# The expert stage of an attention and mixture-of-experts kernel: its convolution-kernel chunks in nine steps instead of eight, the exponential a step later, expert numbers read ahead

## The chip, the core and the metric

The kernel runs on one core of a Trainium2 chip. A core has five engines with a queue of instructions each: TensorE (PE in the profile; PEld is its weight load), VectorE (DVE), ScalarE (ACT), GpSimd (POOL) and SyncE (SP, which here only issues DMAs). They wait for one another by semaphores. The metric is the time of one execution in microseconds on the device; less is better.

## The reference, cut to what matters

Two layers, each a cross attention and a mixture of experts, on x of shape (2, 1024, 256). The stage that the change touches holds the experts of layer 0 (1) and, in the same loop, the convolution kernel K of the state-space part of layer 1 (2), which depends on parameters alone.

```python
# (1) two of eight experts for each of 2048 tokens
topk_val, topk_idx = jax.lax.top_k(gate_scores, TOP_K)
...
for e in range(E):
    h = jnp.einsum('btd,hd->bth', x, W1[e]) + b1[e]
    a, b = jnp.split(h, 2, axis=-1)
    g = a * jax.nn.sigmoid(b)
    eo = jnp.einsum('bth,dh->btd', g, Wo) + bo
    out = out + eo * comb[..., e:e + 1]
# (2) 256 channels, 64 states, 1024 positions
dtA = dt[:, None] * A
dC = C * (jnp.exp(dtA) - 1.0) / A
powers = jnp.exp(dtA[:, :, None] * jnp.arange(L))
K = 2.0 * jnp.einsum('dn,dnl->dl', dC, powers).real
```

## The kernel before

The program is written out engine by engine; the order in each queue is the order of the code, and nothing is scheduled.

**Expert steps.** The 4096 token-expert pairs are sorted by expert and padded to ST = 39 tiles of 128 rows. Each engine runs a loop over `st`, in which step u = st handles tile u:

- GpSimd gathers the rows of tile st from scr_z in device memory by an indirect DMA (line 1554; two buffers, so it waits until TensorE has turned tile st - 2). Then it scatters the gated rows of tile u = st - 4 to scr_g (line 1563), for which it waits for VectorE's product of that tile. At each even st from 4 to 34 it also multiplies and adds a bias to one tile of X (lines 1574 and 1576, the bias pair). At st = 27 it clears VW (a memset).
- TensorE reads the expert number of the tile from teI into a register (`value_load`, line 737), waits for ScalarE's copy of the turned rows and, two steps back, for VectorE's product (g_ready), runs six matmuls into two banks, and then turns (transposes) the gathered tile u + 2 (line 727), for which the gather must have landed.
- ScalarE takes the sigmoid of one bank (line 1261) and copies the turned tile u + 2 (line 1097).
- VectorE multiplies the other bank by it (line 2061), the gating product. It writes one of two buffers, so it also waits until the scatter of tile u - 2 has landed.

**Convolution kernel.** Between these steps K is built in KCH = 4 chunks. With `c, part = (st - KOFF) // KPARTS, (st - KOFF) % KPARTS` each engine does some part of chunk c in step st; before, KOFF = 2 and KPARTS = 8. Before the first chunk VectorE computes coefficients in three blocks (`more_coefficients`). In each chunk:

- parts 0 and 1: VectorE computes two arrays of angles (turns, four operations each). ScalarE takes two sines of each array in parts 1 and 2 (lines 1275 and 1276);
- GpSimd's part 5 writes the arguments of the exponentials, two products (line 1584). GpSimd's st runs some three steps ahead of the others, since it gathers ahead. It waits until the small products of the chunk before are done;
- part 3: ScalarE takes the two exponentials (line 1281);
- parts 4 to 7: VectorE multiplies sines, exponentials and coefficients, ten products, the last at line 2101;
- parts 0 and 1 of the next chunk: TensorE runs the small products, 128 matmuls with tiles of 64 by 32 in each of two halves, behind the expert step and its turn. ScalarE copies each half to KT in that step; the second half needs the first copied, since they use one bank.

Sigmoid, sine and exponential have different tables in ScalarE: each change between them is a load (ACT_TABLE_LOAD at the line of the function that follows). Chunk 0's small products stand at st = 10, 11, those of chunk 3 at st = 34, 35.

**Behind the loop.** SyncE waits for all eight halves to be copied and writes KT to scr_k (line 436), then waits for the last scatter and loads the gated rows from scr_g, four MB-sized pairs (line 311); VectorE sums each tile's two rows, TensorE turns and projects them. TensorE in the meantime computes the film products, which also wait until the eight halves are copied.

Of the kernel before, what the change touches and what calls it, by code (L numbers as in the profile page):

```python
# [29 lines left out]
NE, HID0 = 8, 512  # L30
# [10 lines left out]
FLOOR = -0.5 + 1.0 / 512  # L41
KCH, KPARTS = 4, 8
KOFF = 2
KW = 32
# [41 lines left out]
def build(nc, d, out, last="F"):  # L86
    ctx = ExitStack()
    with ctx:
# [394 lines left out]
        def _(pe):  # L483
# [206 lines left out]
            if "B" in stages:  # L690
# [41 lines left out]
                turn_x(1)  # L732
                pe.wait_ge(s["te_ready"], 1)
                for st in range(max(ST, KOFF + KCH * KPARTS + 2)):
                    if st < ST:
                        u = st
                        e = pe.value_load(teI[0:1, u:u + 1], min_val=0, max_val=NE - 1)
                        pe.wait_ge(s["xTg_sb"], u + 1)
                        if u >= 2:
                            pe.wait_ge(s["g_ready"], u - 1)  # L740
                        for half in range(2):
                            cols = slice(half * HID0, (half + 1) * HID0)
                            o = bank(2 * (u % 2) + half)

                            mm(o, picked[:, u:u + 1].broadcast_to([BROWS, P]), b1r[:, cols], True, False)
                            for k in range(KD):
                                ins = mm(o, xTg[:, u % 2, k, :],
                                         w1all[:, k, bass.ds(e, 1), cols].rearrange("p o n -> p (o n)"), False, k == KD - 1)
                        ins.then_inc(s["h_ps"], 1)
                        if u + 2 < ST:  # L750
                            turn_x(u + 2)
# [341 lines left out]
        def _(a):  # L1093
# [129 lines left out]
            if "B" in stages:  # L1223
# [31 lines left out]
                for st in range(max(ST, KOFF + KCH * KPARTS + 2)):  # L1255
# [15 lines left out]
                    if 0 <= c < KCH and part in (1, 2):  # L1271
# [5 lines left out]
                            .then_inc(s["k_sin"], 1)  # L1277
                    if 0 <= c < KCH and part == 3:
                        a.wait_ge(s["kv_arg"], 2 * c + 2)
                        for mag in (Pr, Qr):  # L1280
                            a.activation(mag, mag, ACT.Exp).then_inc(s["mag_ready"], 1)
# [185 lines left out]
        def _(p):  # L1467
# [72 lines left out]
            if "B" in stages:  # L1540
# [9 lines left out]
                for st in range(ST + SCAT):  # L1550
# [26 lines left out]
                    c, part = (st - KOFF) // KPARTS, (st - KOFF) % KPARTS  # L1577
                    if 0 <= c < KCH and part == 5:

# [139 lines left out]
        def _(v):  # L1719
# [128 lines left out]
            if "B" in stages:  # L1848
# [206 lines left out]
                for st in range(max(ST, KOFF + KCH * KPARTS)):  # L2055
# [17 lines left out]
                    if c >= KCH:  # L2073
                        continue
                    if st in (1, 4, 5):
                        more_coefficients((1, 4, 5).index(st))
                    if c < 0:
                        continue
                    if part < 2:
                        ang = tk[2 * part]  # L2080
                        tts(quads(ang), chan(TURN, c), ramps[:, part, :].unsqueeze(1).unsqueeze(1).broadcast_to([P, 2, 16, R]), ALU.mult)
                        turns4(ang, tk[2 * part + 1]).then_inc(s["k_trig"], 1)
                    elif part == 4:
                        v.wait_ge(s["k_sin"], 2 * c + 2)
# [4 lines left out]
                        tts(flat(Pr), flat(Pr), tk[1], ALU.mult)  # L2089
                    elif part == 5:  # L2090
                        tt(quads(tk[0]), quads(flat(Pi)), chan(17, c), ALU.mult)
                        tt(quads(tk[1]), quads(flat(Pr)), chan(17, c), ALU.mult)
                        v.tensor_tensor(flat(Qr), flat(Qr), tk[3], ALU.mult).then_inc(s["k_used"], 1)
                        own.settle()
                    elif part == 6:
                        tt(quads(flat(Pr)), quads(flat(Pr)), chan(16, c), ALU.mult)
                        tt(quads(flat(Pi)), quads(flat(Pi)), chan(16, c), ALU.mult)
                        own.settle()
                    elif part == 7:
                        tts(flat(Pr), flat(Pr), tk[0], ALU.subtract)  # L2100
                        v.tensor_tensor(flat(Pi), flat(Pi), tk[1], ALU.add).then_inc(s["k_used"], 1)
# [548 lines left out]
```

## Time and profile before

| | us |
|---|---|
| median of 3 runs (765.82 to 771.96) | 769.88 |
| the profiled execution | 768.24 |
| its span from first to last instruction | 766.4 |
| busy: TensorE / VectorE / GpSimd / ScalarE | 662.7 / 542.7 / 381.5 / 313.4 |
| the expert loop, from the first expert matmul to the last | 175.8 to 375.4 |

The profile gives for each instruction its start in us from the start of the span, its length, the line of the code, what it writes and reads, and for the time in which its engine stood idle before it the instruction that ended the wait. "issue" is a wait for nothing that the profile shows. A timeline merges repeats (x128).

### The profile page before, as it was taken

How to read it: one execution, taken by the hardware profiler on the slowest of the kernel's cores; microseconds unless marked ns; L12 is line 12 of the kernel's file. 1: busy time of each engine (PE TensorE's matmuls, PEld its weight loads, DVE VectorE, ACT ScalarE, POOL GpSimd, SP SyncE). 2: the span in 40 equal slices, each digit the busy share in tenths (PEclk: the TensorE clock that was granted, in tenths of full speed). 3: DMA queues.
4: the chain of work that ended last, by engine and by line, in shares of the span. 5: the costliest groups of instructions: out<-in, count | busy, mean ns of one | idle time of the engine just before them, and what ended most of it. 6: DMA issues, size and time to landing. Idle time of an engine off the chain costs nothing.

```text
span 766.4 us, 10944 instructions
## 1 busy us (share of the span) xinstructions
PE 662.7 (86%) x3432; PEld 375.1 (49%) x3432; DVE 542.7 (71%) x1678; ACT 313.4 (41%) x690; POOL 381.5 (50%) x463
## 2 busy tenths in 40 slices
PE   5779998728999999999988779978997999899993
PEld 3434545614445354545467534434543654657672
DVE  5878885393994765744468899999975994745472
ACT  2645764302827465462122467777113220031411
POOL 3777775024988787874213457887300210212130
PEclk9979998657999999999999989999799999999997
DMA  7950001012122212212496000110100000000011
GB/s 216 335 195 18 28 1 56 28 55 69 62 83 84 82 65 83 85 63 88 133 378 254 2 0 2 62 50 0 56 0 0 2 0 1 0 0 1 1 55 56
DMA packets 32958, 52.67 MB, mean 69 GB/s; under 512 B 8712, under 2 KB 21451, under 8 KB 32645
## 3 DMA queue, kind: packets, MB, share of 16 engines
q1 hardware_dynamic: 27620, 36.36, 14.2%
q0 software_dynamic: 4992, 15.34, 5.8%
q8 instruction: 29, 0.48, 0.3%
q10 hardware_dynamic: 288, 0.26, 0.1%
q14 instruction: 29, 0.23, 0.1%
HBM read 36.48 MB, written 15.47 MB: 68 GB/s over the span
## 4 chain that ended last, share of the span: by engine, by line
PE 48%; DVE 29%; ACT 8%; POOL 6%; issue 5%; DMA 3%; SPq 1%; DVEq 0%; POOLq 0%; ACTq 0%
PE ps L485 43%; DVE arena L2236 6%; DVE arena L2226 4%; DVE arena L1723 4%; DVE kp L1723 2%; POOL arena L1528 2%; ACT L1261 2%; PE ps L544 1%; DVE arena L2061 1%; ACT arena L1097 1%; DMA arena<-scr_g 1%; DVE arena L345 1%; PE ps L797 1%; ACT L1275 1%; DVE arena L1998 1%
## 5 line engine op out<-in xcount | busy, mean ns | idle before, releaser
L485 PE MATMUL ps<-arena 64*32 64x32 f32 (+10 forms) x2346 | 478.0, 391 | 19.2 <-DVE arena L1998 8.7
L485 PEld LDWEIGHTS ps<-arena 64*32 64x32 f32 (+7 forms) x2346 | 227.0, 151 | 201.4 <-issue 159.4
L1097 ACT ACTIVATE arena<-ps 128x512 f32<-128x512 f32 (+4 forms) x253 | 121.1, 494 | 239.0 <-PE ps L485 116.0
L340 POOL TENSOR_SCALAR rstd<-mv 128x1 f32<-128x1 f32 (+2 forms) x33 | 13.1, 397 | 218.5 <-DVE mv L334 164.6
L2061 DVE TENSOR_TENSOR arena<-ps,arena 128x512 f32<-128x512 f32 x39 | 26.9, 689 | 76.9 <-ACT arena L1261 75.1
L1563 POOL DMA_INDIRECT scr_g<-arena,destU x39 | 49.5, 1269 | 37.4 <-DVE arena L2061 28.2
L1554 POOL DMA_INDIRECT arena<-scr_z,idsU x39 | 49.1, 1259 | 22.7 <-PE ps L727 10.8
L1261 ACT ACTIVATE arena<-ps 128x512 f32<-128x512 f32 x39 | 23.3, 598 | 85.6 <-PE ps L485 85.4
L2236 DVE MATCH_REPLACE8 arena<-arena 128x77 f32<-128x77 f32 x256 | 53.9, 219 | 0.0
L1417 ACT ACTIVATE arena<-ps,b1p 128x512 f32<-128x512 f32 x32 | 22.0, 687 | 74.3 <-PE ps L485 74.3
L2226 DVE MAX8 arena<-arena 128x8 f32<-128x77 f32 x256 | 41.5, 222 | 1.1 <-ACT arena L1307 1.1
L1723 DVE TENSOR_TENSOR arena<-arena 128x1024 f32<-128x1024 f32 (+8 forms) x44 | 40.2, 913 | 0.9
L1723 DVE TENSOR_TENSOR arena<-arena,kp 128x1024 f32<-128x1024 f32 (+1 forms) x36 | 39.4, 1113 | 0.6
L1528 POOL TENSOR_TENSOR arena<-arena 128x616 f32<-128x616 f32 x32 | 38.9, 1218 | 0.0
L485 PE MATMUL ps<-b1r,picked 73*128 73x512 bf16 x78 | 30.4, 389 | 9.1 <-DVE arena L2061 4.7
L544 PE MATMUL ps<-ident,arena 128*128 128x128 f32 (+1 forms) x160 | 25.7, 294 | 12.1 <-POOL arena L1528 8.0
L1820 DVE TENSOR_REDUCE arena<-ps 128x8 f32<-128x616 f32 x32 | 25.2, 787 | 11.9 <-PE ps L485 11.5
L485 PE MATMUL ps<-wof,arena 128*128 128x256 f32 x128 | 30.8, 386 | 0.0
L342 POOL TENSOR_TENSOR rstd<-rstd,neghalf 128x1 f32<-128x1 f32 (+2 forms) x33 | 29.2, 886 | 2.8
L544 PEld LDWEIGHTS ps<-ident,arena 128*128 128x128 f32 (+1 forms) x160 | 17.4, 144 | 25.9 <-POOL arena L1528 13.0
L1188 ACT ACTIVATE arena<-arena 128x616 f32<-128x616 f32 x32 | 22.9, 715 | 11.9 <-DVE arena L1824 11.9
L345 DVE TENSOR_SCALAR arena<-X,mv,rstd 128x256 f32<-128x256 f32 x48 | 19.3, 454 | 11.2 <-POOL rstd L342 11.2
(223 smaller groups left out, 995.1 us busy)
## 6 DMA issues: line engine op xcount, KB each, us to landing
arena<-in_w1t SPq DMA_DIRECT2D x8, 1024.0 KB, 13.8
arena<-scr_g SPq DMA_DIRECT2D x8, 1024.0 KB, 8.1
scr_z<-arena SPq DMA_DIRECT2D x4, 512.0 KB, 2.9
arena<-in_c_dftf SPq DMA_DIRECT2D x1, 2048.0 KB, 16.0
arena<-in_L_xattn_W SPq DMA_DIRECT2D x2, 1024.0 KB, 6.3
out<-X SPq DMA_DIRECT2D x14, 128.0 KB, 1.8
X<-in_x SPq DMA_DIRECT2D x2, 512.0 KB, 4.8
X<-in_x SPq DMA_DIRECT2D x1, 1024.0 KB, 7.6
```

Source lines behind the costliest of these rows:

```text
L342: p.tensor_tensor(rstd[:, at:at + n], rstd[:, at:at + n], neghalf[:, 0:n], ALU.pow).then_inc(s[signal], 1)
L485: return pe.matmul(o, l, r, start=first, stop=final)
L544: ins = pe.transpose(o, Pb[:, u % PBUF, c * P:c * P + m], ident[:])
L1097: return a.activation(o, i, ACT.Copy)
L1261: a.activation(sig[:, u % 2, :], bank(2 * (u % 2) + 1), ACT.Sigmoid).then_inc(s["sig_ready"], 1)
L1528: p.tensor_tensor(pv, pv, smA[:, u % PBUF, :].unsqueeze(2).broadcast_to([P, HG, S2]), ALU.mult)\
L1554: p.indirect_dma_start(xg[:, st % 2, :], None, scr_z, bass.IndirectOffsetOnAxis(ap=idsU[:, st:st + 1], axis=0))\
L1563: p.indirect_dma_start(scr_g, bass.IndirectOffsetOnAxis(ap=destU[:, u:u + 1], axis=0), gt[:, u % 2, :], None).then_inc(s[f"gs{u % 2}"], 16)
L1723: own.done(v.tensor_tensor(o, x, y, op))
L2061: v.tensor_tensor(gt[:, u % 2, :], bank(2 * (u % 2)), sig[:, u % 2, :], ALU.mult).then_inc(s["g_ready"], 1)
L2226: own.done(v.max(top[:, par, h, 8 * r:8 * r + 8], hv(cur)[:, h, :]))
L2236: ins = v.match_replace(hv(Rr)[:, h, :], top[:, par, h, 8 * r:8 * r + 8], hv(cur)[:, h, :], TAKEN)
```

## The change

Three edits to the loop, and the coefficients' places go with them.

1. KPARTS goes from 8 to 9 and KOFF from 2 to 1. Chunk c begins at st = 1 + 9c instead of 2 + 8c. The small products of chunks 0 to 3 follow their step at st = 10, 19, 28, 37 (first halves) and 11, 20, 29, 38; before, 10, 18, 26, 34 and 11, 19, 27, 35. The coefficients move from st = 1, 4, 5 to 0, 3, 4.
2. The exponentials move from part 3 to part 4, GpSimd's arguments from part 5 to 6, VectorE's products from parts 4 to 7 to parts 5 to 8. The sines stay in parts 1 and 2.
3. TensorE reads the next step's expert number behind its own expert matmuls, in front of the turn and the small products.

```diff
-KCH, KPARTS = 4, 8
-KOFF = 2
+KCH, KPARTS = 4, 9
+KOFF = 1
...
+                def expert_of(u):
+                    return pe.value_load(teI[0:1, u:u + 1], min_val=0, max_val=NE - 1)
+
+                following = expert_of(0)
                 for st in range(max(ST, KOFF + KCH * KPARTS + 2)):
                     if st < ST:
                         u = st
-                        e = pe.value_load(teI[0:1, u:u + 1], min_val=0, max_val=NE - 1)
+                        e = following
...
                         ins.then_inc(s["h_ps"], 1)
+                        if u + 1 < ST:
+                            following = expert_of(u + 1)
                         if u + 2 < ST:
                             turn_x(u + 2)
...
-                    if 0 <= c < KCH and part == 3:
+                    if 0 <= c < KCH and part == 4:
                         a.wait_ge(s["kv_arg"], 2 * c + 2)
...
-                    if 0 <= c < KCH and part == 5:
+                    if 0 <= c < KCH and part == 6:
 
                         p.wait_ge(s["kp_par"], 1)
...
-                    if st in (1, 4, 5):
-                        more_coefficients((1, 4, 5).index(st))
+                    if st in (0, 3, 4):
+                        more_coefficients((0, 3, 4).index(st))
...
-                    elif part == 4:
+                    elif part == 5:
                         v.wait_ge(s["k_sin"], 2 * c + 2)
...
-                    elif part == 5:
+                    elif part == 6:
...
-                    elif part == 6:
+                    elif part == 7:
...
-                    elif part == 7:
+                    elif part == 8:
```

GpSimd's queue at the arguments of chunk 1, before, from the gather at st = 15 on (arena<-scr_z is a gather, scr_g<-arena a scatter; the line numbers are those of the kernel before):

```order
L1554 DMA arena<-scr_z,idsU 128x256
L1563 DMA scr_g<-arena,destU 9088x512
L1584 TENSOR_TENSOR arena<-kp,ramps 128x1024 x2
L1554 DMA arena<-scr_z,idsU 128x256
L1563 DMA scr_g<-arena,destU 9088x512
L1574 TENSOR_SCALAR arena<-rows,cw 128x256
L1576 TENSOR_TENSOR X<-X,arena 128x256
L1554 DMA arena<-scr_z,idsU 128x256
```

The same stretch after the change, whose line numbers are 7 or more higher:

```order
L1561 DMA arena<-scr_z,idsU 128x256
L1570 DMA scr_g<-arena,destU 9088x512
L1561 DMA arena<-scr_z,idsU 128x256
L1570 DMA scr_g<-arena,destU 9088x512
L1581 TENSOR_SCALAR arena<-rows,cw 128x256
L1583 TENSOR_TENSOR X<-X,arena 128x256
L1591 TENSOR_TENSOR arena<-kp,ramps 128x1024 x2
L1561 DMA arena<-scr_z,idsU 128x256
```

The two products of the arguments moved behind one more gather and scatter and behind a bias pair. In chunk 0 they stay where they are, at st = 7.

ScalarE's queue in chunk 1, before, from the copy of a turned tile (128x256) in part 2 on, between the two sine pairs:

```order
L1097 ACTIVATE arena<-ps 128x256
L1275 ACT_TABLE_LOAD
L1275 ACTIVATE arena<-arena 128x1024
L1276 ACTIVATE arena<-arena,halfpi 128x1024
L1261 ACT_TABLE_LOAD
L1261 ACTIVATE arena<-ps 128x512
L1097 ACTIVATE arena<-ps 128x256
L1281 ACT_TABLE_LOAD
L1281 ACTIVATE arena<-arena 128x1024 x2
L1261 ACT_TABLE_LOAD
L1261 ACTIVATE arena<-ps 128x512
L1097 ACTIVATE arena<-ps 128x256
```

After the change:

```order
L1104 ACTIVATE arena<-ps 128x256
L1282 ACT_TABLE_LOAD
L1282 ACTIVATE arena<-arena 128x1024
L1283 ACTIVATE arena<-arena,halfpi 128x1024
L1268 ACT_TABLE_LOAD
L1268 ACTIVATE arena<-ps 128x512
L1104 ACTIVATE arena<-ps 128x256
L1268 ACTIVATE arena<-ps 128x512
L1104 ACTIVATE arena<-ps 128x256
L1288 ACT_TABLE_LOAD
L1288 ACTIVATE arena<-arena 128x1024 x2
L1268 ACT_TABLE_LOAD
```

The exponentials (the line with x2) stand behind one more sigmoid and copy; the loads in front of the two sine pairs have not moved against the sigmoids there.

TensorE's queue at step 10 and the first small products, before, from the step's last matmul on (32x32 x64 is how the small products stand here):

```order
L485 MATMUL ps<-arena 128x512
L727 MATMUL ps<-ident,arena 128x128 x2
L485 MATMUL ps<-arena 32x32 x64
L737 TENSOR_LOAD teI
L737 ISA x2
L485 MATMUL ps<-b1r,picked 128x512
```

After the change:

```order
L485 MATMUL ps<-arena 128x512
L736 TENSOR_LOAD teI
L736 ISA x2
L727 MATMUL ps<-ident,arena 128x128 x2
L485 MATMUL ps<-arena 32x32 x64
L485 MATMUL ps<-b1r,picked 128x512
```

The read of the expert number (TENSOR_LOAD) moved from behind the small products to in front of the turn.

## Rows read from the trace of the kernel before

**Rows 1.** Busy us (count) of PE, PEld, DVE, ACT, POOL in two stretches.

```profile
237.00:255.30 18.30, 16.73 (x48) 7.75 (x48) 5.79 (x8) 18.12 (x21) 13.57 (x12) 1.00 0.21 73
255.30:269.30 14.00, 12.82 (x37) 5.70 (x37) 13.86 (x14) 2.84 (x7) 12.50 (x9) 1.00 0.21 75
```

**Rows 2.** Timeline, PE: start us, length us, instruction, idle before and its releaser.

```profile
228.02 2.23 PE L485 MATMUL ps<-arena 64*32 64x32 f32 x128 [0.77 <-DVE arena L2101]
230.53 0.38 PE L485 MATMUL ps<-b1r,picked 73*128 73x512 bf16 x1 [0.27 <-issue]
...
237.24 0.38 PE L485 MATMUL ps<-b1r,picked 73*128 73x512 bf16 x1 [0.28 <-issue]
...
241.35 0.38 PE L485 MATMUL ps<-b1r,picked 73*128 73x512 bf16 x1
...
255.35 0.38 PE L485 MATMUL ps<-b1r,picked 73*128 73x512 bf16 x1 [1.23 <-DVE arena L2061]
...
269.30 2.23 PE L485 MATMUL ps<-arena 64*32 64x32 f32 x128 [0.72 <-DVE arena L2101]
...
355.13 3.20 PE L485 MATMUL ps<-arena 128*128 x4 [0.60 <-issue]
...
373.49 1.88 PE L485 MATMUL ps<-arena 128*128 x4
```

**Rows 3.** Timeline, ACT, of the same chunk.

```profile
237.01 1.07 ACT L1097 ACTIVATE arena<-ps 64x512 f32<-64x512 f32 x1 [1.52 <-PE ps L485]
238.09 1.28 ACT L1275 ACT_TABLE_LOAD   x1
...
241.50 1.28 ACT L1261 ACT_TABLE_LOAD   x1
...
249.27 1.28 ACT L1281 ACT_TABLE_LOAD   x1
...
252.59 1.28 ACT L1261 ACT_TABLE_LOAD   x1
```

**Rows 4.** Timeline, DVE, of the same chunk.

```profile
254.51 0.69 DVE L2061 TENSOR_TENSOR arena<-ps,arena 128x512 f32<-128x512 f32 x1 [4.81 <-ACT arena L1261]
...
267.86 1.38 DVE L2101 TENSOR_TENSOR arena<-arena 128x1024 f32<-128x1024 f32 x1
```

**Rows 5.** Timeline, POOL, of the same chunk.

```profile
240.44 3.92 POOL L1584 TENSOR_TENSOR arena<-kp,ramps 128x1024 f32<-128x1024 f32 x2
...
245.83 0.99 POOL L1563 DMA_INDIRECT scr_g<-arena,destU  x1 [0.31 <-issue]
246.86 0.95 POOL L1574 TENSOR_SCALAR arena<-rows,cw 128x256 f32<-128x256 f32 x1
...
248.77 1.03 POOL L1554 DMA_INDIRECT arena<-scr_z,idsU  x1 [0.15 <-issue]
...
255.48 1.72 POOL L1563 DMA_INDIRECT scr_g<-arena,destU  x1 [3.08 <-DVE arena L2061]
...
266.94 1.68 POOL L1574 TENSOR_SCALAR arena<-rows,cw 128x256 f32<-128x256 f32 x1
...
269.99 1.90 POOL L1554 DMA_INDIRECT arena<-scr_z,idsU  x1 [0.16 <-issue]
```

**Rows 6.** DMA issues of the page: KB each, median us from issue to landing.

```profile
scr_k<-arena SPq DMA_DIRECT2D x4, 256.0 KB, 5.0
...
arena<-scr_z,idsU POOLq DMA_INDIRECT x39, 3.2
```

**Rows 7.** Busy us by stretch as in rows 1, then PEclk, DMA share, GB/s.

```profile
356.00:357.00 1.00, 1.00 (x2) 0.34 (x1) 0.00 (x0) 0.00 (x0) 0.00 (x0) 0.50 0.34 135
```

**Rows 8.** Timeline, SPq (SyncE's queue of DMA issues) and DVE, end of the experts.

```profile
364.21 4.50 SPq L436 DMA_DIRECT2D scr_k<-arena  x4
379.89 17.48 SPq L311 DMA_DIRECT2D arena<-scr_g  x8
...
388.30 0.49 DVE L1726 TENSOR_SCALAR arena<-arena,cw 128x512 f32<-128x512 f32 x1 [2.65 <-DMA arena<-scr_g]
```

## The prediction

> **What bounds it now.** I first read the busy shares of the expert stage in stretches [rows 1], cut at the three places where the limiting engine changes. One chunk of the convolution kernel lasts from one first half of its small products to the next, 228.02 to 269.30 [rows 2]: 41.28 us for eight expert steps, and three such periods stand in the stage. From 237 to 255.3 ScalarE is busy 18.12 of 18.30 us; from 255.3 to 269.3 VectorE 13.86 of 14.00 and GpSimd 12.50. TensorE is nearly full everywhere, but a step costs it only 4.11 us with its turn (237.24 to 241.35) and a half of the small products 2.23 [rows 2]. Below, C is the start of a first half, and steps are counted from the expert step in front of it, step 0: in the chunk shown step 0 is st = 10 of the code, step 4 is st = 14. What is called a loop index is st itself.
>
> ScalarE [rows 3] copies the second half out (237.01, 1.07), does the first sine pair with its table load (238.09 to 241.50: 3.41), a sigmoid with load and copy, the second pair and another sigmoid (241.50 to 249.27: 7.77, so 2.18 for each sigmoid), the exponentials with their load (249.27 to 252.59: 3.32), and one more load of 1.28, so that the sigmoid of step 4 starts at 253.9, C+25.9. VectorE's gating product of that step starts at 254.51 [rows 4], and TensorE's step 6 waits 1.23 for it [rows 2]. VectorE then works without a pause up to the end of its last product, 254.51 to 267.86+1.38: 14.7 us, and the next small products start right behind it. So each chunk pays a ScalarE queue and a VectorE queue one behind the other. GpSimd waits once, 3.08 us at its scatter of step 4 [rows 5].
>
> **What changes, in numbers.** Removed: nothing; the counts of matmuls, table loads, products and DMAs stay. All is in the order.
>
> *First chunk.* The coefficients and the turns start a step earlier. GpSimd's argument keeps its place, loop index 7, in chunk 0, so the gathers stay where they are. TensorE waited 0.77 for VectorE in front of the first half at 228.02 [rows 2]; the coefficients no longer stand in front of the products that end there, so this goes, and so does one issue gap like the 0.27 in front of 230.53. I take -1 us; bounds 0 (the wait becomes one for a gather) and -2 (twice that, if VectorE's earlier steps had pushed others).
>
> *Steady chunk without GpSimd.* The expert number is read behind the step's matmuls, under cover of the array's work, so the 0.27 in front of 230.53 [rows 2] goes; the second half ends at C+2.23+4.2+2.23 = C+8.7. If it were exposed somewhere else, it would cost the same 0.27 a step, 10 us over 39 steps at worst; I see no such place, since the array has several matmuls queued there. ScalarE: copy 1.07, sines 3.41, load 1.28, so the sigmoid of step 2 starts at C+14.5 and its product is ready at C+15.9. After a second pair the sigmoid of step 3 starts at C+20.1, and step 5 still waits about 0.5. Now no exponential stands in front of step 4's sigmoid: it starts at C+21 instead of C+25.9. The exponentials run C+22 to C+25.3, step 5's sigmoid at C+26.6. Its product and the 14.7 us behind it end at C+41.9. TensorE alone needs C+8.7 and eight steps of 4.11, C+41.6, with the wait C+42.1. So nine steps would take 42.2, against 46.4 for nine at the old pace.
>
> *GpSimd in that chunk.* This is what I expect to take part of it back. Its arguments (240.44, 3.92) now stand at loop index 16: no longer behind the scatter of step 1 but behind the scatter of step 2 and a bias pair. That scatter needs the product that the sines delay, C+15.9; it starts at C+16.1. From there GpSimd has no pause: scatter and bias pair 2.94 (245.83 to 248.77), arguments 3.95, a gather (1.03), a scatter (0.99) and a gather with 0.3 in front of each DMA, 3.9 in all, and the scatter of step 4 starts at C+26.9, hardly before the old C+27.46. In the old trace it was 14.5 us from that scatter to the start of the gather of index 21 (255.48 to 269.99), which took 1.90 [rows 5]; all of a gather lands 3.2 us after issue by the median [rows 6], and I put 3.7 here, since this one is 0.9 longer than the short 1.03. So it lands at C+45.1, and the turn of step 9, after which the small products now come, ends at C+45.5. Before, that gather was needed a step after the products. The arguments themselves are ready at C+23, just in time for the exponentials, which need them at C+23.3. The first period is thus 45.5, not 42.2. The second has one bias pair less there but VW's memset: 45. In the third the bias pairs run out at loop index 34, and 42.2 stands.
>
> The price of a GpSimd instruction is the open one: the bias multiply took 0.95 at 246.86, while VectorE was idle, and 1.68 at 266.94, while it ran products of two tensors [rows 5]. [...] By the short prices the stretch of 14.5 shrinks to 3 scatters and 2 gathers at 1.3 and 2 pairs at 1.9, 10.3 us, the gather lands by C+41 and GpSimd doesn't bind: 42.2. By the long ones (1.9 for each of the DMAs, 3.05 for a pair as from 266.94 to 269.99) it is 17, and a period is 48. I take the measured 14.5, since the same VectorE products lie beside it again.
>
> *End of the stage.* The last first half stands in step 37 instead of 34, so from C only 2.23 and 4.0 are left to the end of step 38: 6.2. Old: 228.02 to 373.49+1.88 = 375.4, 147.4 us. New: 45.5+45+42.2+6.2 = 138.9. Of the 8.5, some 2 are a spell at half clock in the old trace, which I don't repeat: four matmuls took 3.20 at 355.13, against 1.88 at 373.49, with 0.50 granted [rows 2, 7], so 1.3 more in that half of a step, and I count 2 for the step with its gaps.
>
> *Tail.* The kernel's write-out to scr_k is issued when the last half is copied. It took SyncE 4.50 us at 364.21, under cover of the last steps [rows 8]. Now that half follows step 38: ready 2.25 (products) + 1.1 (copy) after the step's end, issued until 7.9 after it. Behind it on SyncE stands the load of the gated rows, which before was issued 4.5 after the end (379.89). So it is at least 3.4 late. The rows of scr_k, 256 KB in 5.0 by the median [rows 6], still run into that load; both bounds: 3.4 (no collision) and 7.3 (the load moves nothing until the last of the four writes has landed, 5.0 behind an issue at 6.8). I take 4.5, nearer the lower end, since only the last write overlaps. The Trainium skill (DMA: Bandwidth & Descriptors, Specifications) wants pieces of 512 B for full rate, and these are 256 B; scr_k's 5.0 for 256 KB agrees. At the rate of the gated load there would be no collision, and the sum 1 us lower. VectorE's first sum (388.30, behind 2.65 us of waiting for that load) moves with it, so all of it is on the path. The film products on TensorE move too, by 2.7, and have cover: they ended well before 388.
>
> **Sum.** -1 - 8.5 + 4.5 = -5.0 on the profiled execution's 768.24: 763.2. The median of the three runs, 769.88, stands 1.6 above it; with that, 764.9. I say 765.0.
>
> **Rivals.**
> *GpSimd does not bind* (chance 0.25). For it: GpSimd still waits 3.08 in each chunk now [rows 5]. Against: 12.50 of 14.00 busy in the VectorE stretch. Periods of 42.2: another 6.1 off, 758.8 on the median's scale.
> *Slower: TensorE loses its clock in the new waits* (0.09). Place: the turn in front of the small products, where it waits about 3 us for the gather in two chunks. In the old trace the granted clock was at 0.50 (1.2 of 2.4 GHz) in the stretch at 356, after a step broken by gaps behind small products [rows 2, 7]. One such fall cost about 2 us there. Three of them eat the 5.0, and with them ScalarE's queue starts later too; six make it over 1% slower. Against: the waits of 1.23 within steps did not lower it.
> *It does not do what it says* (0.08): the sines, which stay back to back, hold the period, the exponential only moves ScalarE's load from one step to the next, and TensorE's saving is returned by the tail: 768 to 771.
>
> **Chances.** The forecast has 0.58, within 762 to 769. A measurement of this kernel can tell about 1%, 7.7 us. Faster by more, below 762.2: nearly all of the first rival and a little of the forecast's edge, 0.27. Slower, above 777.6: half of the second rival, 0.05. The rest, 0.68, is within 1%. Range 757 to 772: from the first rival with the short tail to long GpSimd prices in both chunks (+5) and a tail of 6.5 to 7.3.
>
> **What would show it.** Right: three periods between first halves, of about 45.5, 45 and 42; ScalarE's sigmoid of the fourth step some 5 us earlier after C; TensorE's longest idle times in front of the turn before a first half, released by the gather; GpSimd's arguments right behind a scatter and bias pair that waited for VectorE; no issue gap behind small products; SyncE's gated load 8 us behind the last expert step. Wrong: periods of 42 (GpSimd was mispriced); idle TensorE released by VectorE's last product (ScalarE and VectorE still bind); granted clock of 0.50 inside the stage; the first sum no later after the last step than now, 13 us.

## The result, and the profile after the change

| us | before | after | predicted |
|---|---|---|---|
| median of 4 runs beside each other | 769.20 (765.82 to 771.96) | 778.33 (775.82 to 781.59) | 765.0 (757 to 772) |
| the profiled execution, its span | 768.24, 766.4 | 779.91, 778.1 | 763.2 |
| first small products of chunk 0 | 228.02 | 227.30 | 227.0 |
| the three periods from there | 41.28, 41.06, 41.13 | 47.70, 48.31, 44.13 | 45.5, 45, 42.2 |
| last first half to the end of the last gating product | other order | 10.74 | 7.56 |
| from there to the first sum | 11.57 | 17.66 | 16.1 |
| the first sum | 388.30 | 395.84 | 383.3 |

The ratio is 1.011, with a 95% interval of 1.007 to 1.015: slower, and outside my range. The last column is worked out from the prediction's terms: 6.2 plus the 1.36 by which the last product ended behind TensorE before (376.04 + 0.69 against 373.49 + 1.88), 11.57 plus 4.5, and 388.30 less 5.0. The miss at the first sum is 12.5 us: 0.3 in the start, 7.4 in the periods, 3.2 in the last steps, 1.6 in the tail.

Timeline of PE after the change (columns as in [rows 2]):

```profile
205.73 0.38 PE L485 MATMUL ps<-b1r,picked 73*128 73x512 bf16 x1 [3.10 <-DVE arena L2068]
...
227.30 2.24 PE L485 MATMUL ps<-arena 64*32 64x32 f32 x128
...
248.79 0.38 PE L485 MATMUL ps<-b1r,picked 73*128 73x512 bf16 x1 [0.51 <-DVE arena L2068]
...
274.63 0.44 PE L727 MATMUL ps<-ident,arena 128*128 128x128 f32 x2 [3.17 <-DMA arena<-scr_z,idsU]
275.00 2.77 PE L485 MATMUL ps<-arena 64*32 64x32 f32 x124
...
279.11 3.62 PE L485 MATMUL ps<-arena 128*128 x4
...
285.06 2.23 PE L485 MATMUL ps<-arena 64*32 64x32 f32 x128
...
318.60 0.44 PE L727 MATMUL ps<-ident,arena 128*128 128x128 f32 x2 [2.08 <-DMA arena<-scr_z,idsU]
...
367.44 3.00 PE L485 MATMUL ps<-arena 64*32 64x32 f32 x128 [1.93 <-DVE arena L2108]
370.37 0.61 PE L485 MATMUL ps<-b1r,picked 73*128 73x512 bf16 x1
370.77 3.62 PE L485 MATMUL ps<-arena 128*128 x4
```

The first period ends with a turn, at 274.63, that waits 3.17 for the gather, as I had said; but the four matmuls at 279.11 behind it then take 3.62 instead of 1.88. The third ends with a first half, at 367.44, that waits 1.93 for VectorE's last product (L2108), and the same follows. The busy time by stretch (columns as in [rows 1], then PEclk, DMA share, GB/s) shows why:

```profile
255.30:275.00 19.70, 14.69 (x44) 6.52 (x42) 13.68 (x13) 3.32 (x7) 17.66 (x11) 1.00 0.19 66
...
274.60:286.00 11.40, 10.77 (x201) 6.80 (x202) 5.95 (x6) 2.32 (x4) 8.94 (x7) 0.70 0.28 96
...
367.40:378.50 11.10, 11.06 (x247) 7.16 (x249) 1.28 (x2) 1.63 (x2) 1.01 (x2) 0.69 0.07 27
```

GpSimd is busy 17.66 of 19.70 us and TensorE 14.69; before it was 12.50 and 12.82 of 14.00 [rows 1]. Behind the two waits the granted clock is 0.70 and 0.69 on average, so part of each stretch ran at 1.2 of 2.4 GHz. From 275.00 to the second half at 285.06 it is 10.06 us, where chunk 0 took 6.36 (227.30 to 233.66): 3.7 for one fall.

ScalarE is where I had put it: the sigmoid of step 4 at C+20.8 (248.09), the exponentials at C+23.0, step 5's sigmoid at C+26.3.

```profile
248.09 0.60 ACT L1268 ACTIVATE arena<-ps 128x512 f32<-128x512 f32 x1
...
250.28 2.00 ACT L1288 ACTIVATE arena<-arena 128x1024 f32<-128x1024 f32 x2
...
253.59 0.60 ACT L1268 ACTIVATE arena<-ps 128x512 f32<-128x512 f32 x1
```

GpSimd (POOL) in the same chunk, and the VectorE products that run beside it:

```profile
243.33 1.00 POOL L1570 DMA_INDIRECT scr_g<-arena,destU  x1 [1.99 <-DVE arena L2068]
...
253.94 0.99 POOL L1570 DMA_INDIRECT scr_g<-arena,destU  x1 [0.30 <-issue]
254.97 2.92 POOL L1581 TENSOR_SCALAR arena<-rows,cw 128x256 f32<-128x256 f32 x1
257.98 1.12 POOL L1583 TENSOR_TENSOR X<-X,arena 128x256 f32<-128x256 f32 x1
259.25 2.03 POOL L1561 DMA_INDIRECT arena<-scr_z,idsU  x1 [0.15 <-issue]
261.59 1.93 POOL L1570 DMA_INDIRECT scr_g<-arena,destU  x1 [0.30 <-issue]
...
266.13 2.95 POOL L1581 TENSOR_SCALAR arena<-rows,cw 128x256 f32<-128x256 f32 x1
...
270.96 1.84 POOL L1561 DMA_INDIRECT arena<-scr_z,idsU  x1 [0.16 <-issue]
```

```profile
254.83 1.22 DVE L1730 TENSOR_TENSOR arena<-arena 128x1024 f32<-128x1024 f32 x1
255.96 1.22 DVE L1736 SCALAR_TENSOR_TENSOR arena<-arena 128x1024 f32<-128x1024 f32 x1
257.21 1.30 DVE L1730 TENSOR_TENSOR arena<-arena 128x1024 f32<-128x1024 f32 x1
...
266.02 2.35 DVE L1730 TENSOR_TENSOR arena<-arena,kp 128x1024 f32<-128x1024 f32 x2
268.40 0.69 DVE L2068 TENSOR_TENSOR arena<-ps,arena 128x512 f32<-128x512 f32 x1
```

The scatter of step 4 starts at C+26.6 (predicted 26.9). From it to the gather of index 21 it is 17.0 us (253.94 to 270.96), not the 14.5 of before [rows 5]: the bias multiply now meets the first of VectorE's products and takes 2.92, where before the scatter met them (1.72) and the multiply came behind it (1.02). The rows of before, POOL and DVE:

```profile
257.25 1.02 POOL L1574 TENSOR_SCALAR arena<-rows,cw 128x256 f32<-128x256 f32 x1
```

```profile
256.25 1.22 DVE L1729 SCALAR_TENSOR_TENSOR arena<-arena 128x1024 f32<-128x1024 f32 x1
257.50 1.38 DVE L1723 TENSOR_TENSOR arena<-arena 128x1024 f32<-128x1024 f32 x1
```

That multiply also had a product of VectorE beside it (257.50) and was quick all the same. What the rows have in common is a short break between two of VectorE's instructions: each multiply ends 0.7 to 0.8 us behind the first such break after its start (before: 257.47 and, with [rows 4] and [rows 5], 267.86; after: 257.18 and 268.37). So its time goes by how far off that break is. This is read from four rows; no run tests it.

VectorE in front of the last first half, the scaling of VW's bias row at loop index ST - 3 (L1733, mgate), and the end of the experts (columns as in [rows 8]):

```profile
362.86 1.28 DVE L1733 TENSOR_SCALAR arena<-arena,mgate 1x2048 f32<-1x2048 f32 x1
364.18 0.69 DVE L1733 TENSOR_SCALAR arena<-arena 1x1024 f32<-1x1024 f32 x1
364.90 1.22 DVE L1730 TENSOR_TENSOR arena<-arena 128x1024 f32<-128x1024 f32 x1
366.16 1.22 DVE L2108 TENSOR_TENSOR arena<-arena 128x1024 f32<-128x1024 f32 x1
...
377.49 0.69 DVE L2068 TENSOR_TENSOR arena<-ps,arena 128x512 f32<-128x512 f32 x1 [9.50 <-ACT arena L1268]
...
395.84 0.49 DVE L1733 TENSOR_SCALAR arena<-arena,cw 128x512 f32<-128x512 f32 x1 [6.38 <-DMA arena<-scr_g]
```

The last gating product of before, and SyncE's queue (SPq) after:

```profile
376.04 0.69 DVE L2061 TENSOR_TENSOR arena<-ps,arena 128x512 f32<-128x512 f32 x1 [3.18 <-ACT arena L1261]
```

```profile
380.27 4.49 SPq L436 DMA_DIRECT2D scr_k<-arena  x4
384.89 20.98 SPq L311 DMA_DIRECT2D arena<-scr_g  x8
```

The row's 1.97 us stand in front of the last two products. The gated load starts 6.71 behind the last gating product (378.18 to 384.89; before 3.16), and the first sum 10.95 behind the load's issue (before 8.41).

### The profile page after: what moved, and what is told of

Read it like the earlier page. It is cut to its first block, busy times and chain, and to the rows that moved or that the text cites. A ratio compares the mean times of both kernels' runs of the same rounds, so it can differ in the third digit from the quotient of the medians.

```text
span 778.1 us, 10945 instructions
## 1 busy us (share of the span) xinstructions
PE 667.3 (86%) x3432; PEld 379.5 (49%) x3432; DVE 547.8 (70%) x1678; ACT 313.3 (40%) x690; POOL 383.3 (49%) x463
## 4 chain that ended last, share of the span: by engine, by line
PE 49%; DVE 26%; POOL 11%; ACT 5%; issue 5%; DMA 3%; SPq 1%; DVEq 0%; POOLq 0%; ACTq 0%
PE ps L485 44%; DVE arena L2243 6%; DVE arena L2233 4%; DVE arena L1730 2%; DVE kp L1730 2%; POOL arena L1535 2%; PE ps L544 1%; DVE arena L345 1%; POOL arena L1581 1%; POOL arena L1561 1%; DMA arena<-scr_g 1%; PE ps L804 1%; POOL scr_g L1570 1%; ACT arena L1104 1%; DVE arena L1733 1%
## 5 line engine op out<-in xcount | busy, mean ns | idle before, releaser
L485 PE MATMUL ps<-arena 64*32 64x32 f32 (+10 forms) x2346 | 484.7, 396 | 19.5 <-DVE arena L2005 8.7
L485 PEld LDWEIGHTS ps<-arena 64*32 64x32 f32 (+7 forms) x2346 | 232.3, 154 | 204.8 <-issue 163.0
L1104 ACT ACTIVATE arena<-ps 128x512 f32<-128x512 f32 (+5 forms) x253 | 121.0, 494 | 253.0 <-PE ps L485 117.8
L1570 POOL DMA_INDIRECT scr_g<-arena,destU x39 | 46.2, 1184 | 33.9 <-DVE arena L2068 25.6
L1561 POOL DMA_INDIRECT arena<-scr_z,idsU x39 | 48.1, 1234 | 25.4 <-PE ps L727 13.6
L544 PE MATMUL ps<-ident,arena 128*128 128x128 f32 (+1 forms) x160 | 25.4, 292 | 14.5 <-ACT arena L1104 7.5
L485 PE MATMUL ps<-wof,arena 128*128 128x256 f32 x128 | 33.2, 408 | 0.0
L544 PEld LDWEIGHTS ps<-ident,arena 128*128 128x128 f32 (+1 forms) x160 | 17.2, 142 | 28.3 <-issue 16.4
## 6 DMA issues: line engine op xcount, KB each, us to landing
arena<-in_w1t SPq DMA_DIRECT2D x8, 1024.0 KB, 14.5
```

The source lines that it names most:

```text
L485: return pe.matmul(o, l, r, start=first, stop=final)
L544: ins = pe.transpose(o, Pb[:, u % PBUF, c * P:c * P + m], ident[:])
L1104: return a.activation(o, i, ACT.Copy)
L1561: p.indirect_dma_start(xg[:, st % 2, :], None, scr_z, bass.IndirectOffsetOnAxis(ap=idsU[:, st:st + 1], axis=0))\
L1570: p.indirect_dma_start(scr_g, bass.IndirectOffsetOnAxis(ap=destU[:, u:u + 1], axis=0), gt[:, u % 2, :], None).then_inc(s[f"gs{u % 2}"], 16)
```

## The experiments

Twelve kernels. *Periods* are those between first halves; *end* is from the last first half to the end of the last gating product (only where the small products stand as in the changed kernel); *sum* is from there to the first sum. Ratios are to the kernel before on the same chip (its medians were 771.9 to 773.1).

| kernel | periods | end | sum | ratio (95%) |
|---|---|---|---|---|
| e1 before, read-ahead alone | 40.9, 40.8, 41.0 | | 11.9 | 0.998 (0.996 to 1.001) |
| e13 before, write-out late | 41.3, 42.8, 41.1 | | 18.5 | 1.011 (1.006 to 1.015) |
| e6 changed, again | 48.1, 48.7, 44.3 | 10.8 | 17.3 | 1.008 (1.005 to 1.012) |
| e9 changed, thin bias pair | 42.1, 42.1, 43.9 | 10.7 | 17.8 | 0.992 (0.989 to 0.996) |
| e11 changed, narrow products | 42.3, 42.1, 42.3 | 7.6 | 17.2 | 0.989 (0.986 to 0.992) |
| e2 changed, arguments early | 42.1, 46.7, 44.1 | 9.2 | 17.7 | 1.000 (0.998 to 1.003) |
| e14 e2 and VW cleared late | 42.1, 42.7, 43.9 | 9.3 | 17.8 | 0.992 (0.988 to 0.995) |
| e4 changed, row later | 48.0, 48.7, 42.4 | 7.6 | 18.0 | 1.001 (0.998 to 1.005) |
| e3 changed, write-out behind | 48.1, 48.6, 44.2 | 10.8 | 11.8 | 0.996 (0.991 to 1.000) |
| e10 exponential back | 45.0, 45.1, 43.4 | 7.6 | 17.5 | 0.999 (0.996 to 1.002) |
| e12 e10 with two cures | 45.0, 48.4, 43.4 | 7.6 | 11.7 | 0.989 (0.986 to 0.992) |
| e8 changed, four cures | 42.1, 42.7, 41.9 | 7.6 | 11.4 | 0.984 (0.981 to 0.988) |

### The changed kernel again (e6)

No edit; it ran beside e8, e9 and e10.

> The changed kernel once more, beside the others of this set. Expected by every theory: ratio to before 1.008 to 1.015, periods between first halves of 47 to 48.5, 47.5 to 49 and about 44. If the two long periods came out below 46, they would have been an accident of one profile and not of the order.

779.02 against 772.41; both long periods, both falls of the clock and the long tail are there again. So they belong to the order of the kernel, and not to one profile.

### GpSimd's queue: a thin bias pair (e9), narrow products (e11)

e9 leaves GpSimd's two bias instructions in place, on one column:

```diff
-p.tensor_scalar(bof[:, T % 2, :], rows[:, BOF, :], cw[:, NSEL, T:T + 1], None, ALU.mult)
+p.tensor_scalar(bof[:, T % 2, 0:1], rows[:, BOF, 0:1], cw[:, NSEL, T:T + 1], None, ALU.mult)
-p.tensor_tensor(X[:, T, :], X[:, T, :], bof[:, T % 2, :], ALU.add)
+p.tensor_tensor(X[:, T, 0:1], X[:, T, 0:1], bof[:, T % 2, 0:1], ALU.add)
```

> The changed kernel with the bias pair on 1 of its 256 columns: the bias of the other 255 is left out of the output, and GpSimd's two instructions of a pair fall from some 4 to 5 us to a few tenths. Nothing else moves. Theory (GpSimd's queue from the scatter of step 4 on is what the late gather stands behind): periods of 42 to 43, 42 to 44 and 44, no wait for a gather in front of a first half, 5 to 10 us less than the changed kernel, ratio to before 0.997 to 1.004. Rival (the late products of ScalarE and VectorE hold the scatters back, and GpSimd only follows): periods stay at 46 to 48, ratio 1.007 to 1.015.

The wait for the gather is gone, the first two periods are 42.1, the third keeps its 43.9: GpSimd's queue is what the long periods stand behind. Timeline of PE in e9, to be held against 274.63 above:

```profile
272.02 0.38 PE L727 MATMUL ps<-ident,arena 128*128 128x128 f32 x2
272.33 2.24 PE L485 MATMUL ps<-arena 64*32 64x32 f32 x128
```

The total fell by more than I had expected (0.992; expected 0.997 to 1.004): against e6 the two periods alone give 12.6 us, and the fall of the clock behind the first wait went with it.

e11 leaves GpSimd as it is and narrows VectorE's ten products of a chunk, like this one:

```diff
-tt(flat(Pi), flat(Pr), tk[0], ALU.mult)
+tt(flat(Pi)[:, 0:64], flat(Pr)[:, 0:64], tk[0][:, 0:64], ALU.mult)
```

> The changed kernel with VectorE's ten products of a chunk on 64 or 128 of their 1024 columns; the other columns of K are left out of the output (two clearings of 128x1024 on VectorE before the first products keep them finite). GpSimd's queue is untouched. Theory (GpSimd's bias multiply of 128x256 takes 2 to 3 us only because VectorE's products of two tensors run beside it): every bias multiply from the second chunk on takes 0.95 to 1.1, the scatters and gathers 1.0, the stretch from the scatter of step 4 to the gather of index 21 falls from 17.0 to 11 to 13 us, no wait for a gather in front of a first half, periods of 42 to 43, 8 to 12 us less than the changed kernel, ratio to before 0.994 to 1.001. Rival (the price is GpSimd's own, of the work behind a scatter): bias multiplies at 2 to 3 us stay, and so do the waits for the gather.

Timeline of POOL in e11, the same chunk from the scatter of step 4 to the gather of index 21:

```profile
257.70 0.99 POOL L1570 DMA_INDIRECT scr_g<-arena,destU  x1 [0.30 <-issue]
258.74 1.02 POOL L1581 TENSOR_SCALAR arena<-rows,cw 128x256 f32<-128x256 f32 x1
...
265.69 0.94 POOL L1581 TENSOR_SCALAR arena<-rows,cw 128x256 f32<-128x256 f32 x1
...
267.62 1.04 POOL L1561 DMA_INDIRECT arena<-scr_z,idsU  x1 [0.15 <-issue]
```

The scatter of step 4 starts at C+26.6 again (C is 231.09 here). The same multiplies take 1.02 and 0.94 instead of 2.92 and 2.95, a scatter or gather about 1.0, and the stretch of 17.0 is 9.9 (257.70 to 267.62, shorter than I had expected), though no GpSimd instruction was touched. So the price is the overlap with VectorE. Since VectorE's own queue is shorter here too, the third period lost its wait as well; the total (0.989, below the 0.994 to 1.001 that I had expected) is therefore no measure of the overlap alone. The periods of 42 without a late gather can be read from both kernels.

### The places of arguments and clearing (e2, e14)

e2 moves GpSimd's arguments one step up, e14 also the clearing of VW:

```diff
-                    if 0 <= c < KCH and part == 6:
+                    if 0 <= c < KCH and part == 5:
...
-                    if st == 27 and "C" in stages:
+                    if st == 36 and "C" in stages:
```

> The changed kernel with GpSimd's two argument products one loop index earlier (part 5 again), so in front of the scatter that waits for the product delayed by the sines. Theory (these products stand in the loop from one first half over sines, scatter and gathers to the next): the first two periods shrink from 47.7 and 48.3 by about 4 us each, the wait for the gather in front of the first halves at step 19 (3.17 us) goes or falls under 1, and the whole comes to about 770. Rival 1 (GpSimd is bound by its work as a whole, wherever the arguments stand): periods stay above 47, 777 to 779. Rival 2 (the falls of TensorE's clock make the loss): periods shrink only where no fall to 0.50 is left.

> The changed kernel with two of the four places moved: GpSimd's arguments at part 5 and VW cleared at loop index 36 instead of 27. The row and the write-out stay as changed. Theory (the clearing of 1.8 us is what kept the second period at 46.7 when only the arguments were moved): periods 42.1, 42.1 to 43 and 44, about 4 us less than with the arguments alone (ratio 1.000), so 0.993 to 0.997. Rival (the bias pairs hold the second period): 42.1, 45.5 to 46.7 and 44, ratio 0.998 to 1.002.

e2: first period 42.1, but the second 46.7, with a wait of 2.56 for a gather and a fall of the clock behind it (0.58 from 311 to 315). Timeline of PE in e2:

```profile
310.35 0.44 PE L727 MATMUL ps<-ident,arena 128*128 128x128 f32 x2 [2.56 <-DMA arena<-scr_z,idsU]
...
310.85 3.48 PE L485 MATMUL ps<-arena 128*128 x4
```

e14: 42.1 and 42.7, and neither the wait nor the fall. The arguments behind the scatter that waits for the sine-delayed product cost the first period; in the second the clearing, 1.8 us on GpSimd at loop index 27, does as much. By the ratios e2 gained 0.8% on e6 and e14 0.9% on e2, across chips.

### The row in front of the last products (e4)

```diff
-                    if st == ST - 3 and "C" in stages:
+                    if st == ST - 2 and "C" in stages:
```

> The changed kernel with VectorE's scaling of the bias row (1.28 and 0.69 us on one partition) one step later, so behind and not in front of the last two products of the last chunk. Theory (these 2 us were hidden before and now stand in front of the last first half): the third period falls from 44.1 to about 42.2 and the whole by 2 us, 776.3; if the fall of the clock at that place goes with the wait of 1.93, up to 4 us, 774. Rival (GpSimd or the tail has the slack): third period shorter, whole unchanged at 778.

The third period is 42.4 instead of 44.1 to 44.3, and the end 7.6 instead of 10.7 to 10.8, with a granted clock of 1.00 from 370.0 to 377.7. Two instructions of 1.97 us together cost 5 us in the trace: 1.9 as a wait, 3.2 by the clock behind it.

### The tail alone (e13), and cured (e3)

e13 is the kernel before; only its write-out is issued later, in front of the first gated load:

```diff
                 sp.wait_ge(s["k_sb"], 2 * KCH)
-                for j in range(4):
-                    sp.dma_start(scr_k...[:, :, j * NS:(j + 1) * NS], ...).then_inc(s["k_out"], 16)
                 sp.wait_ge(s["xbA"], NT)
...
+                for j in range(4):
+                    sp.dma_start(scr_k...[:, :, j * NS:(j + 1) * NS], ...).then_inc(s["k_out"], 16)
                 load_gated(0)
```

> The kernel before with one edit: the write-out to scr_k is issued when the last scatter has landed, directly in front of the first gated load, instead of some 15 us earlier. The experts are untouched. Theory (the tail term alone, 4.5 us of issue in front of the gated load and some 2.5 of transfer beside it): gated load 4.6 later against the last gating product than before (7.8 instead of 3.2), first sum 6.5 to 7.5 later against it, ratio 1.006 to 1.011. Rival (only the issue counts, or the sums have slack behind the first one): first sum 4.5 later or less, ratio 1.0 to 1.005.

Timeline of SPq and of DVE in e13:

```profile
380.10 4.49 SPq L445 DMA_DIRECT2D scr_k<-arena  x4
384.64 20.76 SPq L311 DMA_DIRECT2D arena<-scr_g  x8
```

```profile
395.38 0.49 DVE L1726 TENSOR_SCALAR arena<-arena,cw 128x512 f32<-128x512 f32 x1 [9.59 <-DMA arena<-scr_g]
```

The experts end as before (last product 376.87; the clock fell at 272 here, and not at 355). The gated load is issued 7.77 behind it instead of 3.16, and the first sum comes 10.74 behind the issue instead of 8.41: 4.6 of issue and 2.3 of a slower load. The whole kernel is 1.05% slower. So the 6.9 us of this place (4.6 and 2.3) show in the time of the whole kernel; nothing behind the first sum absorbs them.

e3 puts the same four writes behind the first two gated loads of the changed kernel:

```diff
+                load_gated(0)
+                load_gated(1)
                 for j in range(4):
                     sp.dma_start(scr_k...[:, :, j * NS:(j + 1) * NS], ...).then_inc(s["k_out"], 16)
-                load_gated(0)
-                load_gated(1)
```

> The changed kernel with the write-out to scr_k behind the first two loads of gated rows on SyncE's queue. Theory (the load is late by the 4.5 us of issuing and by sharing the DMA engines): the gated load is issued 3.2 us behind the last gating product instead of 6.7, the first sum starts 8.4 behind it instead of 11.0, and the whole is 5 to 6 us faster, 773. Rival (the write only moves behind and delays the load of the kernel and the normalisation, which wait for it): the first sum is earlier, but the whole is the same, 777 to 779.

The first sum is 11.8 behind the last product, as before the change, with the long periods unchanged. By the trace that is 5.9 us; the ratio against e6's says some 10, on another chip and with an interval of 0.4% on either side. But one of e3's ten runs, at 761.05, lies 8.5 us below the next: by the medians of all runs (772.25 against 773.12, and e6's 779.02 against 772.41) it is some 7.5. What is left is not explained.

### The read-ahead alone (e1)

The diff's third edit on the kernel before.

> The kernel before with one edit only: the expert number is read behind the step's own expert matmuls. Theory (the read was exposed behind the small products and in front of steps that wait for nothing else): the issue gaps of about 0.27 us behind the eight halves go, at most 2 us, 767 to 769. Rival (the periods are set by ScalarE, VectorE and GpSimd, so TensorE's gaps have cover): no change, 769. If the read were harmful (it delays the turn): above 771.

The periods are 0.1 to 0.4 shorter. The gaps behind the small products are gone, and the first two first halves wait 1.17 and 1.16 for VectorE's last product instead of 0.77 and 0.72 [rows 2]. The ratio is no measurable change.

### What the exponential's place is worth (e10, e12)

e10 puts back what part 3 to part 7 did, within nine steps (the arguments at part 5):

```diff
-                    if 0 <= c < KCH and part == 4:
+                    if 0 <= c < KCH and part == 3:
                         a.wait_ge(s["kv_arg"], 2 * c + 2)
...
-                    elif part == 5:
+                    elif part == 4:
                         v.wait_ge(s["k_sin"], 2 * c + 2)
```

> The changed kernel with only the exponential put back: exponentials at part 3, GpSimd's arguments at part 5, VectorE's products at parts 4 to 7, so that of nine steps the last has no product of the convolution kernel. Nine steps, the early start and the read-ahead stay. Theory (the ninth step is the gain, the later exponential adds nothing to it but puts GpSimd's and VectorE's work closer together): periods of 42 to 43.5, a wait of about 1.2 within each chunk at the sixth step, none in front of a first half, also not in the third chunk, since the row's scaling comes behind the last product; 766 to 771 where before is 770, ratio 0.995 to 1.002. Rival (the exponential's place is what makes nine steps pay): step 4 late as before, periods 45 to 47, ratio 1.004 to 1.012.

My periods of 42 to 43.5 were wrong for two of the three: they are 45.0 and 45.1, as the rival had it, at a ratio that was mine. Most of the time lies in the wait of step 6 and in one for the gather (timeline of PE in e10):

```profile
251.09 0.38 PE L485 MATMUL ps<-b1r,picked 73*128 73x512 bf16 x1 [1.23 <-DVE arena L2068]
268.72 0.44 PE L727 MATMUL ps<-ident,arena 128*128 128x128 f32 x2 [0.98 <-DMA arena<-scr_z,idsU]
```

Yet the clock stayed at 1.00 behind both, and the total is 1% below the changed kernel's. e12 adds the two cures that apply (VW cleared at 36, the write-out behind):

> The kernel with the exponential put back (exponentials at part 3, arguments at part 5, products at parts 4 to 7, nine steps), with the two cures that apply to it: VW cleared at loop index 36 and the write-out behind the first two gated loads. It tells what the exponential's later place is worth once GpSimd's queue and the tail are cured. Theory (the exponential in front of step 4's sigmoid costs 1.2 to 1.5 at TensorE's sixth step and puts one more wait at the gather): periods 43.4 to 45, 4 to 9 us above the kernel with the four cures (whose ratio was 0.984), ratio 0.988 to 0.994. Rival (nine steps and the cures are all of the gain): ratio 0.981 to 0.987.

0.989, 5 us above e8's median on another chip. Its second period holds one spell at a lower clock, 0.83 from 274 to 284, behind a wait of 0.96 and with a pause of 1.48 inside the small products that the profile puts down to nothing. There the second half comes 9.6 behind the first instead of 6.36; without that the period is about 45. So by the traces the later exponential is worth 2 to 3 us in each of the first two periods and 1.5 in the third, once what it collides with is out of the way.

### All four cures (e8)

The edits of e14, e4 and e3 together.

> The changed kernel with four places moved: GpSimd's arguments at part 5, the clearing of VW at loop index 36 instead of 27, the scaling of VW's bias row one step later, and the write-out to scr_k behind the first two gated loads. Theory (GpSimd's queue in the two long periods, the row in the third, and the write-out in the tail are all that the change costs): periods 42 to 42.5 three times, no wait over 1.5 us in front of a first half, the gated load about 3.5 and the first sum about 9 behind the last gating product, 755 to 763 where before is 770, ratio 0.98 to 0.99. Rival (a period of 42 only moves the pressure: the second period keeps 46 because of the bias pairs, or the time gained in the experts is given back by a lower granted clock or by the sums behind): ratio 0.993 to 1.0.

759.27 against 772.41, ratio 0.984: the version that beats both kernels. Its end of the experts, by stretch, and the first sum:

```profile
354.70:362.50 7.80, 7.80 (x238) 5.34 (x239) 3.36 (x4) 2.23 (x3) 1.89 (x1) 1.00 0.18 69
```

```profile
373.78 0.77 DVE L1734 TENSOR_SCALAR arena<-arena,cw 128x512 f32<-128x512 f32 x1 [0.16 <-DMA arena<-scr_g]
```

TensorE is busy all through, at full clock, and VectorE hardly waits for the gated load. The first sum comes 11.4 behind the last product, as in e3, and not the 9 that I had expected. 42.1 and 42.7 and 41.9 are the 42.2 that I had worked out for a chunk that GpSimd doesn't bind, and 7.6 is the end that I had worked out without a fall of the clock.

## Why the prediction was wrong, point by point

**The start, near by luck**: C+0 came 0.7 earlier, for -1, but 0.6 of that lies in front of the loop, whose first expert matmul came at 175.21 instead of 175.82. From there to C+0 it is 52.1 us, against 52.2 before. The wait of 0.77 is gone, as I had said; but the coefficients, a step earlier, now stand in front of a gating product, and one of their 128x128 products takes 4.41 (from 199.80), beside GpSimd's arguments (200.28, 3.77), where the median of its like nearby is 0.29. TensorE waits 3.10 for what stands behind it (205.73). I had looked only at what the coefficients no longer delay.

**The steady chunk without GpSimd, right**: ScalarE's places came within 0.3 us of those forecast after C, the scatter of step 2 started at C+16.0 for 16.1 (243.33), step 5's wait was 0.51 for 0.5, and e9, e14 and e8 show 42.1 for 42.2.

**GpSimd's price, mis-sized.** The mechanism was the one named: arguments behind the scatter of step 2, the scatter of step 4 at C+26.6, the late gather in front of the small products. The step that failed is "I take the measured 14.5, since the same VectorE products lie beside it again". The same products did, but other GpSimd instructions met them, at other moments. The stretch took 17.0, my own long bound; a period of 48 was worked out for it, and 47.7 was measured. The row at 257.25, 1.02 beside a product, already showed that products beside an instruction don't set its price by themselves. The Trainium skill (GPSIMD Engine Reference, 1. Specifications) names contention of GpSimd with VectorE's instructions that have two SBUF inputs; the trace agrees, with 0.94 to 1.02 in e11 against 2.92 and 2.95. The trace shows either engine held up: GpSimd here, VectorE in its product of 4.41 beside the arguments.

**The clock, wrongly left out.** I gave 0.09 to a fall of the clock in the new waits, with about 2 us a fall, and said that six would make it slower by over 1%. Two came, of 3.7 and 3.2: one behind the turn that I had named, one behind a wait that I had not seen. With the first, the second period is 48.3; without it 44.6, for my 45. I had sized a fall by the half step that showed it before [rows 2, 7]; these two lasted over the small products and a step or more.

**The third period, a step not seen.** The prediction followed GpSimd's and ScalarE's queues past the moved parts, but not what else stands in VectorE's: the row's scaling at ST - 3 = 36 used to stand behind all products and now, with part 8 of chunk 3 at index 36, in front of the last two. 1.9, and 3.2 by the clock; e4 took back both.

**The tail, right in kind, short in size**: 4.5 predicted, 6.1 measured, within the bounds of 3.4 and 7.3. The issue came 3.55 late, as worked out; the load beside the writes lost 2.5 us instead of 1.1. e13 shows the term by itself.

**The sum.** 2.2 - 0.4 + 1.9 in the periods, 3.7 + 3.2 by the clock, 1.6 in the tail and 0.3 in the start are the 12.5 us of the miss. The rest of the difference of the two spans, 11.7 - 7.5 = 4.2 us behind the first sum, is not put down to the change: e1, whose order of experts and tail is that of before, has it too (its span less the start of its first sum is 384.3 us, after the change 382.3, before 378.1).

That the waits lower the clock is read from where it fell, not shown by an experiment on the clock. Right in front of small products, or of the turn that leads to them, all ten waits of 1.9 to 3.3 had a fall behind them (after, e2, e3, e6, e9, e14, and e4 in its second period). In front of the matmuls of an expert step it was less regular. Four waits of 2.1 to 2.2 stand at the place of 318.60 (after, e3, e4, e6), and only e4's had one (0.58 from 322 to 326); e2's 2.56 had one. Of twelve waits of 2.2 to 3.3 before the small products of chunk 0, like that at 205.73, seven had one. And the clock also fell without a wait over 1.5: in the kernel before at 355, in e13 at 211 and 272 (0.57 from 272 to 276), and in e12. So a long wait isn't needed for a fall, and what else it takes stays open. The gains of the single cures add up to more than e8's; how they divide isn't settled.

## What to carry to other kernels

When a schedule gets a step longer, list for each engine all that was not moved with it (here a clearing, a row's scaling, a write-out, GpSimd's place for the arguments), and see on which side of the moved parts it now lies: four such places stand between a loss of 1% and a gain of 1.6%. A price that was measured beside another engine holds only where the two start at the same moments; where the stretch binds, forecast with its long bound. And a wait in front of many small matmuls can cost more than its length: here the clock fell behind all ten of 1.9 us and more.

## What the runs showed of the hardware that I had not expected

- A 128x256 TENSOR_SCALAR on GpSimd took 0.94 and 1.02 us beside VectorE's narrowed products (e11) and 2.92 and 2.95 at the same places beside its 128x1024 products, three times as much; one that started just ahead of a break between two products took 1.02 (before, 257.25). An indirect DMA issue took 1.0 in e11 and up to 2.03 after the change. The other way round, a 128x128 product of VectorE took 4.41 beside GpSimd's arguments (after, 199.80), where the median nearby was 0.29.
- Four writes of 256 KB, issued ahead of 1 MB loads in the same queue, delayed the first use of those loads by 2.3 (e13) and 2.5 us (after) beyond what their issue did (4.6 and 3.55).
- A TensorE wait of 1.93 us in front of 128 matmuls of 64 by 32 was followed by a granted clock of 0.69 over 11 us, and cost 3.2 us beyond the wait; the same wait cost 1.6 beyond it in e2 (end 9.2 against 7.6).
